# A perceiver layer with eight experts: routing in pairs of groups, and seven of the 23 expert blocks ahead of the others

## What is computed

```python
x = x + xattn(layernorm(x), ctx)     # 64 batches x 32 tokens x 256, against 257 context rows each
x = x + attn(layernorm(x))           # inside each batch of 32 tokens: the 8 most similar earlier tokens
x = x + ffn(layernorm(x))            # 2048 tokens, 8 experts, the best one for each token

# ffn, with x the 2048 normalised tokens
router_probs = softmax(x @ Wr)                       # 2048 x 8
expert_idx = argmax(router_probs); p_max = max(router_probs)
h = gelu(x @ W1[e] + b1[e]);  out = p_max * (h @ W2[e] + b2[e])     # for e = expert_idx of the token
```

## Time and profile before

| | us |
|---|---|
| median of 3 runs | 526.98 (525.98 to 528.96) |
| profiled execution | 528.04, its span 526.1 |
| first 20 us, constants and first loads | 0 to 20 |
| steps 0 to 15 | to 280.3 |
| steps 16 to 19 | 280.3 to 320.2 |
| routing, first gathers | 320.2 to 348.0 |
| 23 expert blocks | 348.0 to 516.1 |
| last store | 516.1 to 526.1 |

### The profile page before, as it was taken

The page is one execution under the profiler, slowest core; times in us unless marked ns, Lnnn a source line. Parts: engine busy times, 40 slices in busy tenths (PEclk is TensorE's granted clock), DMA queues, the critical chain, the costliest instruction groups (busy, mean ns, idle before and its releaser), DMA issues. The chain is left out here.

```text
span 526.1 us, 10389 instructions
## 1 busy us (share of the span) xinstructions
PE 458.0 (87%) x2848; PEld 339.0 (64%) x2849; DVE 272.8 (52%) x794; ACT 267.9 (51%) x580; POOL 206.6 (39%) x377
## 2 busy tenths in 40 slices
PE   4889999999999889999997632169999999999992
PEld 3555555666666456666564421169999999999991
DVE  1456878778787578778776546501222221222110
ACT  2267668877788578777785331023332233322230
POOL 2441235334453155243532210643544455445331
PEclk9999999999999999999997655569999999999997
DMA  8602521435314333263340012466557555566110
GB/s 229 204 30 91 171 91 44 148 112 191 111 50 143 112 107 102 90 190 110 111 162 20 20 41 101 145 234 220 191 209 212 210 162 182 200 219 208 47 21 0
DMA packets 47880, 68.93 MB, mean 131 GB/s; under 512 B 5469, under 2 KB 39839, under 8 KB 47713
## 3 DMA queue, kind: packets, MB, share of 16 engines
q1 hardware_dynamic: 41808, 59.09, 33.9%
q0 software_dynamic: 3312, 8.13, 5.7%
q10 hardware_dynamic: 2720, 1.26, 0.9%
HBM read 62.17 MB, written 7.21 MB: 132 GB/s over the span
## 5 line engine op out<-in xcount | busy, mean ns | idle before, releaser
L1177 PE MATMUL pK<-stage,Wkr 128*128 128x512 f32 x256 | 124.3, 611 | 2.6 <-DVE stage L674 2.0
L340 POOL TENSOR_SCALAR ve<-mv 128x1 f32<-128x1 f32 x48 | 13.7, 286 | 185.5 <-DVE mv L597 185.5
L1369 PE MATMUL b<-W,XF 128*128 x368 | 83.1, 379 | 0.0
L1369 PEld LDWEIGHTS b<-W,XF 128*128 128x128 f32 x368 | 68.2, 190 | 8.4
L1177 PEld LDWEIGHTS pK<-stage,Wkr 128*128 128x128 f32 x256 | 44.5, 193 | 43.0 <-issue 41.7
L964 DVE SCALAR_TENSOR_TENSOR XF<-b,p_slot,XF 128x256 f32<-128x256 f32 x23 | 11.1, 484 | 104.6 <-PE b L1369 104.6
L1015 ACT ACTIVATE stage<-pK,bkr 128x512 f32<-128x512 f32 x64 | 42.8, 689 | 38.1 <-PE pK L1177 38.1
L1110 ACT ACTIVATE XF<-pT,b_now 128x128 f32<-128x128 f32 x96 | 27.3, 370 | 54.4 <-PE pT L1351 54.3
L1110 ACT ACTIVATE XF<-pK,b_now 128x128 f32<-128x128 f32 x88 | 25.2, 369 | 50.6 <-PE pK L1351 50.6
L1022 ACT ACTIVATE stage<-stage 128x512 f32<-128x512 f32 x64 | 40.5, 633 | 14.9 <-DVE stage L669 14.7
L1351 PE MATMUL pT<-XF,stage 128*128 128x128 f32 x384 | 46.6, 282 | 0.0
(11 more groups left out here) (204 smaller groups left out, 762.2 us busy)
## 6 DMA issues: line engine op xcount, KB each, us to landing
stage<-in_L_ffn_W_dram SPq DMA_DIRECT2D x23, 1024.0 KB
stage<-in_ctx_dram SPq DMA_DIRECT2D x32, 512.0 KB, 4.9
W<-in_L_ffn_W_dram SPq DMA_DIRECT2D x8, 1024.0 KB, 6.0
ctx_last<-in_ctx_dram SPq DMA_DIRECT2D x64, 32.0 KB, 3.9
normal_tokens<-xn SPq DMA_DIRECT2D x16, 128.0 KB, 2.9
residual_tokens<-X SPq DMA_DIRECT2D x16, 128.0 KB, 2.7
X<-in_x_dram SPq DMA_DIRECT2D x1, 1792.0 KB, 7.5
stage<-in_L_ffn_b_dram SPq DMA_DIRECT2D x1, 1024.0 KB, 6.6
```

What stands on the lines that cost most here:

```text
L1177: mm = pe.matmul(pK[r][:], Wkr[:, c, r * P:(r + 1) * P], ctx_T[:, c, half * 512:(half + 1) * 512], start=c == 0, stop=c == DC - 1)
L1369: mm = pe.matmul(p_out[b], f_hT[b][:, n * P:(n + 1) * P], W2[:, bass.ds(e, 1), n, :].rearrange("p o d -> p (o d)"), start=n == 0, stop=n = ...
```

## The change

1. **Routing by pairs.** `pair` names pair q of groups (2q, 2q+1) for step 2q+6; the logits of both are there then. In that step VectorE runs `route(q)` (six small instructions, after the moments of `two`), ScalarE one exp, POOL `count_pair` (three small adds), TensorE two small rank matmuls at the end, and VectorE `probability` and `places` (five small ones) behind the logits. In the odd step after it, POOL's first work is `scatter(q)`: two indirect DMAs that write the token numbers into a list per expert in DRAM. A step 20 is added for the last pair. All the old routing, its matmuls and the POOL products are gone.
2. **Rows.** Normalised row, x2 row and probability lie side by side in one DRAM row of 513 floats: one store by SP and one gather by POOL for each block instead of two.
3. **Three waves of blocks.** After 10 groups three blocks, after 14 groups four, and at the end 16 are planned (`plan`, 13 to 17 small VectorE instructions, in steps 15, 19 and 20); 3 and 4 are the numbers of full blocks that these groups always have. SP reads the list's start, loads 128 token numbers for a block, and POOL gathers the rows and later stores by the same numbers.
4. **Where the early blocks run.** A block is four quarters: up first half, up second half, transposes of the next block with down first half, down second half. The table FILL says how many quarters run at which place of which step: 4 in step 16, 4 in 17, 2 in 18, 3 in 19, 15 in 20.
5. **Late blocks.** TensorE's order in block j is now: up of j, transposes of j+1, down of j; one PSUM buffer each for the transposes and the output where there were two. POOL's order is gather(j), store(j-3), where gather(j) waits for the stores up to j-4 to have landed.

The diff, cut to its core:

```diff
+WAVES = ((10, 3), (14, 4), (NG, 16))
+EARLY = sum(n for _, n in WAVES[:-1])
+FIRSTS = [sum(n for _, n in WAVES[:w]) for w in range(len(WAVES))]
+FILL = {(16, "b2"): 1, (16, "c"): 1, (16, "d"): 1, (16, "e"): 1, (17, "a"): 2, (17, "c"): 1, (17, "d"): 1,
+        (18, "a"): 2, (19, "a"): 2, (19, "e"): 1, (20, "e"): 15}
+FIRST_AT = {(16, "b"): 0, (19, "e"): 1}
+def pair(k, parity, kp):
+    q = k - 3
+    if parity or isinstance(q, int) and not 0 <= q < NG // 2:
+        return None
+    return q, 2 * ((kp + 1) % 2)
...
 # GpSimd
+            def scatter(q, r0, turn):
+                s = r0 // 2
+                count = in_register(pool, 16 + 32 * turn)
+                settle(pool, S["consts"])
+                pool.wait_ge(tokens_st[s], count)
+                pool.tensor_copy(token_now[:, r0:r0 + 2], token_all[:, bass.ds(2 * q, 2)]).then_inc(S["token_r"], 1)
+                count = in_register(pool, q + 1)
+                settle(pool, S["consts"])
+                pool.wait_ge(S["place_r"], count)
+                pool.wait_ge(S["token_r"], count)
+                pool.wait_ge(tokens_st[1 - s], 16)
+                for i in range(2):
+                    pool.indirect_dma_start(by_expert, bass.IndirectOffsetOnAxis(ap=place[:, r0 + i:r0 + i + 1], axis=0),
+                                            token_now[:, r0 + i:r0 + i + 1], None).then_inc(tokens_st[s], 16)
...
+            def gather(j):
+                at_least(pool, f_y_st[j % 2], 16 * (j // 2 - 1))
+                pool.wait_ge(token_ld[j % SLOTS], 16 * (j // SLOTS + 1))
...
+                pool.indirect_dma_start(f_row[:, j % SLOTS, :], None, rows,
+                                        bass.IndirectOffsetOnAxis(ap=token_i[:, j:j + 1], axis=0)
+                                        ).then_inc(f_row_ld[j % SLOTS], 16)
...
             def step(k, parity, half, kp):
+                if parity and pair(k, 0, kp):
+                    q, r0 = pair(k, 0, kp)
+                    scatter(q, r0, half - 2 + kp)
+                if isinstance(k, int) and s == 19:
+                    for j in range(FIRSTS[1], FIRSTS[1] + 3):
+                        gather(j)
                 # last key column, rstd of two, of coming, o_norm, rstd of four: as before
...
+                if routed:
+                    count_pair(routed[0])
                 # X + bv, hg: as before
+                if isinstance(k, int) and s == 15:
+                    for j in range(FIRSTS[1]):
+                        gather(j)
+                if isinstance(k, int) and s in (16, 17):
+                    store(s - 16)
+                if isinstance(k, int) and s == 19:
+                    store(2)
+                    gather(FIRSTS[1] + 3)
+            scatter(NG // 2 - 1, (NG - 2) % 4, NG // 4 - 1)
+            store(3)
+            for j in range(EARLY, NBLK):
+                gather(j)
+                store(j - 3)
 # SP, after the last ctx loads
+            load_tokens(0, 0, FIRSTS[1])
+            sp.wait_ge(S["pv"], NG - 1)
+            stream_w1(0, 0, 0)
...
+            stream_w1(1, 1, 0)
+            sp.wait_ge(S["khat_r"], 4 * NG)
+            stream_w1(2, 2, 0)
+            keep(5, 2)
+            keep(6, 0)
+            load_tokens(1, FIRSTS[1], FIRSTS[2])
+            sp.wait_ge(S["pv"], NG)
+            for j in range(FIRSTS[1], EARLY):
+                stream_w1(j, j % SLOTS, j // SLOTS)
+                if j == SLOTS:
+                    keep(7, 2)
+            load_tokens(2, EARLY, EARLY + SLOTS)
 # VectorE, step
                 if two:
                     moments(two[0], st2, mv2, "st2_r", "mv2_r")
+                if routed:
+                    route(routed[0])
                 # y of four, nmaxA of one, h of two: as before
...
+                if isinstance(k, int) and s == 15:
+                    plan(0)
...
                 if four:
                     g, b, _ = four
+                    if routed:
+                        v.wait_ge(S["rank_mm"], routed[0] + 1)
                     v.wait_ge(S["route_mm"], g + 1)
-                    v.tensor_copy(group_of(logits, g), p_route).then_inc(S["logits_r"], 1)
+                    v.tensor_copy(logits[:, b, :], p_route).then_inc(S["logits_r"], 1)
+                if routed:
+                    probability(*routed)
+                    places(*routed, half - 2 + kp)
+                if isinstance(k, int) and s == 20:
+                    plan(2)
+                fill(k, parity, "e")
 # TensorE
+            def quarter(j, i):
+                at = j, j % SLOTS, j // SLOTS
+                if i < 2:
+                    up(*at, i)
+                if i == 2:
+                    if j + 1 not in FIRSTS:
+                        in_T(*following(*at))
+                    down(j, j % SLOTS, (0,))
+                if i == 3:
+                    down(j, j % SLOTS, (1,))
...
+            def late_block(j, q, turn):
+                up(j, q, turn, 0)
+                up(j, q, turn, 1)
+                if not isinstance(j, int) or j + 1 < NBLK:
+                    in_T(*following(j, q, turn))
+                down(j, q, (0, 1))
```

More of the change, by code:

```diff
@@ L240, in perceiver_layer @@
-        expert = sb("expert", [P, NBLK])
+        index_i = sb("index_i", [P, E], I32)
+        index = sb("index", [P, E])
+        base_w = sb("base_w", [P, E], BF16)
+        one8 = sb("one8", [P, E])
+        LATE = WAVES[-1][1]
+        blk_i = sb("blk_i", [P, LATE], I32)
+        blk, blk_rows = sb("blk", [P, LATE]), sb("blk_rows", [P, LATE])
+        count_e, used_e, m_e, c_e, ends, starts, from_e, took = (
+            sb(n, [P, E]) for n in ("count_e", "used_e", "m_e", "c_e", "ends", "starts", "from_e", "took"))
@@ L319, in group_of, with row, filler, fill @@
             return t[:, bass.ds(g, 1), :].rearrange("p o d -> p (o d)")
+        def row(r, lo, hi):
+            return rows_out[:, r, lo:hi]
+        def filler(quarter, first):
+            done = [0]
+            def fill(k, parity, place):
+                if not isinstance(k, int):
+                    return
+                at = (2 * k + parity, place)
+                if at in FIRST_AT:
+                    first(FIRSTS[FIRST_AT[at]])
+                for _ in range(FILL.get(at, 0)):
+                    quarter(done[0] // 4, done[0] % 4)
+                    done[0] += 1
+            return fill
         @block.gpsimd
@@ L506, in _ @@
+            run_steps(pool, step)
+            scatter(NG // 2 - 1, (NG - 2) % 4, NG // 4 - 1)
[3 more added lines that the diff above has]
+                store(j - 3)
+            for j in range(NBLK - 3, NBLK):
+                store(j)
             pool.wait_ge(f_y_st[0], 16 * ((NBLK + 1) // 2))
@@ L587, in _ @@
+            load_tokens(2, EARLY, EARLY + SLOTS)
+            for j in range(EARLY, NBLK):
+                stream_w1(j, j % SLOTS, j // SLOTS)
+                if (j - EARLY) % SLOTS == 0 and j + SLOTS < NBLK:
+                    load_tokens(2, j + SLOTS, j + 2 * SLOTS)
         @block.vector
@@ L678, in step @@
+            fill = filler(quarter, first)
+            def step(k, parity, half, kp):
+                now, one, two, three, four, coming = (groups(k, parity, n) for n in (0, 1, 2, 3, 4, -1))
+                routed, s = pair(k, parity, kp), 2 * k + parity
+                r4 = (2 * kp + parity) % 4
+                fill(k, parity, "a")
+                if isinstance(k, int) and s == 19:
+                    plan(1)
                 if now:
@@ L1242, in step @@
                     at_least(pe, S["logits_r"], g - 3)
+                    if parity and pair(k, 0, kp):
+                        pe.wait_ge(S["place_r"], k - 2)
+                    if isinstance(g, int) and g == 1:
+                        pe.wait_ge(S["b1_cp"], 1)
                     for c in range(CC):
```

702 lines of the change are left out of this document (350 added, 352 removed).

## The result

The changed kernel takes 545.01 us (median of four runs, 542.06 to 548.87) beside 527.97 for the kernel before: a ratio of 1.033, 95% interval 1.029 to 1.038. The profiled execution has a span of 542.9 us. In a later batch the same kernel took 550.6 (548.7 to 555.2) beside 527.6, a ratio of 1.047 (1.041 to 1.053): from batch to batch it moves by over 1%, so a time is compared closely only with the times of its own batch.

The account below looks back on a forecast made before the run. TensorE was taken to bound the steady steps and late blocks, with an underused drain and routing between. Steady pairs +22.0, step 15 +1.2, drain -12.5, late blocks +4 gave a 540.8 us span, 541.7 median, forecast 542, range 507 to 562.

Parts of the forecast that it names:

- Even steps: Steady even steps: route's small VectorE instructions delay h by 1.1 us and rank matmuls add 0.2, together 1.3 (0.2 to 2.0).
- The wait for h in odd steps: Steady odd steps: the scatter ahead of rstd on GpSimd makes TensorE wait 2.65 to 3.6 us, taken as 3.1.
- the lower of the two ways I gave: Odd-step scatter: 0.9 + 1.0 + 1.0 us if the second DMA is prepared under the first, 0.9 more if not.
- The drain: Step 16 to block 7: 107.8 us with 13 block quarters added, against 120.3 for the same work before, gain 12.5.
- The queues named for steps 17 to 19: Drain: new work stands ahead on GpSimd (17), ScalarE (18), VectorE and GpSimd (19); steps of 18.5, 14.5 and 19 us.
- about 3 to land: First gather's path from plan(0) in step 15: SP's list load lands about 3 us after issue, rows ready at 22.
- The late blocks: Last 16 blocks: TensorE needs 7.25 us a block, but GpSimd's round of 8.0 costs 4 us in all (0 to 39).
- My L of 5.3: Late blocks: assumed landing time of a block's store, 5.3 us, which the gather four blocks later waits for.
- Slow indirect DMAs beside a busy VectorE: Steady odd steps: scatters beside busy VectorE cost 5.6 us instead of 3.1, +12.5, giving 554; chance 0.15.
- The late stage follows GpSimd: Late blocks: with store landing at 7 us GpSimd's round is 9.7, 24 us lost instead of 4, 562; chance 0.07.
- The drain really takes the blocks: Drain: quarters fit TensorE's idle time, block 7 starts 71.6 us after step 16; 505, or 483; chance 0.20.
- the 93 from which it decides: Drain: if step 16 to block 7 is shorter than about 93 us, the changed kernel is faster than before.

Follow-up runs that it names:

- the wide kernels: Kernels with token-list entries 64 bytes apart; against the changed kernel with only that altered, 4-byte entries took 535.6 us (1.015), 64-byte entries had ratio 1.011.
- with both mended: Changed kernel plus 64-byte list entries, scatter behind hg and steps 17 to 19 reordered: 513.5 us, ratio 0.970; again 515.1 us, 0.975.
- a drain with one queue mended of two: Changed kernel with GpSimd's gathers 3 to 5 in step 19 put behind the last group's rstd: 548.3 us, ratio 1.037.

## Why the prediction was right, and where it wasn't

The forecast was 542, range 507 to 562, slower at 0.72; measured 545.0. The total is closer than its parts, and that is luck: the odd steps cost more than I had, the steps ahead of them less, and in the drain steps 16 and 18 came out shorter and the others longer. Two slips of mine change nothing: the hole in the slices is 24 to 26, not 22 to 25, and the stages added one by one give 541.3 for the span, not 540.8.

**Even steps: right.** +1.3 expected; three of the five took 17.41 to 17.51 us, +1.0, step 14 16.89. Step 10 has the loop's edge, 19.66.

**The wait for h in odd steps: the path right, the size at the lower end.** I took 3.1 between 2.65 and 3.6. The copy of ctx_T cost 0.27 and h 1.98 to 2.14, together 2.3 to 2.4. The second DMA is prepared under the first, which was the lower of the two ways I gave, and `place` comes 1.54 us into the step instead of my 2.04. The kernel with the scatter behind hg confirms the cause: the waits go to 0.28 to 0.35.

**What was missing in the odd steps.** They took 19.98 to 22.40 us, +3.5 to +6.0. Over the 2.4 that I had seen, two things came: waits for context rows (6.8 us in four steps) and the half clock behind the gap. I priced the scatter's time on GpSimd and never asked when it lands, although the lists' readers wait for just that. The nearest row, a gather's 6.4 us from issue to use, would have been too low: 10.3 to 13.5. The ten steps took 195.4 us against 168.4, +27.0, where my sum had 23.2; the six steps ahead of them ran 2.3 us faster than before, so step 16 came at 304.99 against my 303.5.

**The drain.** By steps 18.9, 20.1, 13.5 and 20.0 (predicted 21, 18.5, 14.5 and 19), and 36.8 to block 7 (34.8): 109.3 against 107.8. The queues named for steps 17 to 19 are those that held it, by their waits of 3.92, 7.69 and 11.90, and each wait fell when its queue was reordered, that of step 17 only from 3.97 to 3.08. One thing was hidden in them: landings of 6.63 and 11.22 us for scatters 6 and 7. My sum had no term for them; its "about 3 to land" was that of a list load.

**The late blocks: loss right, reason half wrong.** 3.2 us lost against 4. GpSimd waited for the store's landing as I said, but its round isn't 8.0. In the quiet part it looks like this, start of a store to the next gather 2.6 us:

```profile
455.60 1.00 POOL L467 DMA_INDIRECT out_dram<-XF,token_i  x1 [2.19 <-DVE XF L862]
458.19 0.98 POOL L461 DMA_INDIRECT f_row<-rows_by_token,token_i  x1 [1.59 <-DMA out_dram<-XF,token_i]
```

while ahead of the six gathers between 411 and 449, at first beside W1 loads that catch up (392 GB/s from 414 to 425), it is 4.6 to 7.2. My L of 5.3 lies between two levels. The estimate of 2.3 us from the Trainium skill's "DMA: Bandwidth & Descriptors", Anatomy of one DMA, lies near the quiet level, 2.6, which has the gather's own start in it. Freed of the wait, the kernel gained at most 2.1 us there; the rest fits the last scatter's landing, since it is gone in the wide kernels, but no run separates it.

**The rivals.** *Slow indirect DMAs beside a busy VectorE* was close in price and wrong in mechanism. Beside VectorE at eight tenths a scatter's instruction takes 1.04 us, in the late stage a gather's 0.98; no scatter is seen to be held up on GpSimd, and with entries 64 bytes apart in the same steps it lands in half the time. The Trainium skill's "SBUF — State Buffer", Who interferes with whom, has VectorE in certain modes and GpSimd shut each other out for a whole instruction. No such stop shows here, and the trace doesn't say which modes VectorE was in, so this case doesn't test the rule. *The late stage follows GpSimd* is out (the kernel without the wait). *The drain really takes the blocks* fell for the changed kernel (109 us, above the 93 from which it decides) by nothing but order and landing: with both mended the way, counted from step 16's scores, is 93.0 us in one profile and 98.5 in the other, where it was 108.5, and the steady steps lose 12.8 and 11.5 instead of 24.8, so the kernel is 2.5 to 3% faster than before. The rival to which I gave 0.20 needed a handful of moved lines and a list 16 times as wide.

Left open: why the clock falls behind some of the gaps and not behind others of the same length, and why words written to neighbouring addresses land late.

## What to carry to other kernels

Price an indirect write twice: what it costs the engine that issues it, and when it lands; who waits for the landing is a chain of its own. Don't scatter small words to neighbouring addresses; spread the entries, here to 64 bytes, and read them with a stride. Work that is moved into an idle stage has to stand behind the chain on every engine's queue that it touches: a drain with one queue mended of two gave 0 us, with all mended and the lists landing early some 20.

## What the runs showed of the hardware

- An indirect DMA that writes 128 words of 4 bytes, those of one expert side by side, lands after 9.2 to 15.7 us in the steady steps, and about 11.9 with idle queues around it; 64 bytes apart after 4.0 to 6.8, and 2.1 to 3.1 with 64-byte entries in a quiet slot.
- Two indirect DMAs in a row cost GpSimd 1.1 + 0.3 + 0.97 us.
- With the second DMA of such a scatter issued 2.7 us before the loop's edge, VectorE stood still for 8.25 and 9.22 us without a wait that the profile names and without traffic; with wide lists in the same order 2.2 to 2.5, and 2.6 in the kernel before. The packet on the instruction queue at the start of the stop took 1.7 to 1.8 us, not 0.3 to 0.5. So its next code seems to be held up with the scatter; the profile doesn't say whose code the packet brought.
- After a gap of 2 us in an odd step TensorE worked on at 0.51 to 0.63 of full clock for some 4 us; behind gaps of the same 1.98 in two other odd steps the mean clock stayed at 1.00.
